# Attention and expert kernel: masked scores kept in SBUF, first weights split in two parts, first x loaded tile by tile

## What is computed

```python
latent = xn @ w_kv_down                      # rank 128
k, v   = split(latent @ w_kv_up)             # 16 heads of 64
q      = xn @ w_q
att    = softmax(causal(q @ k.T / 8))
y      = (att @ v) @ w_out
# ffn: router of 8 experts (top 2 of sigmoid scores), each expert silu(x@g.T)*(x@u.T)@d.T,
# plus one shared expert for all tokens
```

## Time and profile before

| | |
|---|---|
| time, median of 3 | 1002.02 us |
| the profiled execution's own time | 1002.06 us |
| its span, first to last instruction | 1000.3 us |
| PE busy | 957.1 us (96%) |
| DVE, ACT, POOL busy | 727.8, 635.1, 340.7 us |
| mean granted TensorE clock | 0.993 of full |

### The profile page before, as it was taken

How to read it: one execution, slowest core, us unless ns; L and a number is a source line. 1 busy time by engine, 2 the same in 40 slices (tenths; PEclk the granted TensorE clock), 3 DMA queues, 4 the chain that set the end, 5 groups by cost and what they waited for, 6 DMA issues and landing times.

```text
span 1000.3 us, 20204 instructions
## 1 busy us (share of the span) xinstructions
PE 957.1 (96%) x7200; PEld 768.1 (77%) x7200; DVE 727.8 (73%) x2014; ACT 635.1 (63%) x1799; POOL 340.7 (34%) x333
## 2 busy tenths in 40 slices
PE   3879997899999999999999999999999999999998
PEld 2656776678888878888788887888878778777776
DVE  4889699997666666675666656676675786888884
ACT  3746666554767666766666775666756676667772
POOL 0231113223234234442343523445131444444441
PEclk9899999999999999999999999999999999999999
DMA  6486424361324525455244553456433442533421
GB/s 192 164 305 243 161 98 147 126 205 36 135 76 147 185 91 174 123 180 178 101 162 142 180 161 105 153 165 178 152 97 134 161 125 76 180 108 101 132 86 43
DMA packets 65412, 142.78 MB, mean 143 GB/s; under 512 B 7776, under 2 KB 40288, under 8 KB 63520
## 3 DMA queue, kind: packets, MB, share of 16 engines
q1 hardware_dynamic: 52880, 92.19, 27.9%
q0 software_dynamic: 12432, 49.29, 15.8%
HBM read 104.76 MB, written 36.70 MB: 141 GB/s over the span
## 4 chain that ended last, share of the span: by engine, by line
PE 83%; DVE 7%; issue 7%; POOL 1%; DMA 1%; ACT 1%; POOLq 0%; DVEq 0%; SPq 0%
PE PS L667 15%; PE PS L709 14%; PE PS L668 13%; PE PS L669 13%; PE PS L700 13%; PE PS L690 12%; PE PS L816 2%; DVE acc L985 1%; PE PS L808 1%; DVE PS L1240 1%; DMA xs<-xs_scratch 1%; POOL rstd L1345 1%; PE PS L715 1%; DVE ohB L1204 0%; DVE acc L1164 0%
## 5 line engine op out<-in xcount | busy, mean ns | idle before, releaser
L923 ACT ACTIVATE pp<-PS,nmax 128x128 f32<-128x128 f32 (+3 forms) x512 | 263.6, 532 | 130.6 <-DVE nmax L1240 130.4
L1240 DVE CUSTOM_DVE_ANT_0 PS<-PS,maskw 128x128 f32<-128x128 f32 (+3 forms) x512 | 232.3, 522 | 5.0 <-PE PS L690 5.0
L1396 POOL TENSOR_TENSOR yy<-yf,yy 128x512 fp32r<-128x512 f32 x63 | 82.4, 1307 | 287.2 <-ACT yy L853 287.2
L700 PE MATMUL PS<-ident,pp 128*128 128x128 f32 x1280 | 165.2, 275 | 0.3 <-DVE qk L1137 0.2
L690 PE MATMUL PS<-qk 64*128 64x256 f32 (+2 forms) x1536 | 147.1, 337 | 12.8 <-DVE qk L1226 11.0
L700 PEld LDWEIGHTS PS<-ident,pp 128*128 128x128 f32 x1280 | 141.3, 141 | 15.4 <-issue 9.3
L709 PE MATMUL PS<-pt,vv 128*64 128x512 f32 (+3 forms) x1024 | 152.0, 439 | 0.1
L709 PEld LDWEIGHTS PS<-pt,vv 128*64 128x64 f32 x1024 | 67.8, 136 | 90.4 <-issue 72.3
L690 PEld LDWEIGHTS PS<-qk 64*128 64x128 f32 x1536 | 114.2, 190 | 28.8 <-issue 10.7
L853 ACT ACTIVATE pt<-PS 128x384 f32<-128x384 f32 (+1 forms) x215 | 108.7, 512 | 3.3 <-PE PS L700 3.1
L1246 DVE COPY pt<-PS 128x384 f32<-128x384 f32 x169 | 99.7, 591 | 12.7 <-PE PS L700 12.7
(11 more groups left out here) (169 smaller groups left out, 2075.0 us busy)
## 6 DMA issues: line engine op xcount, KB each, us to landing
rb<-rr_scratch SPq DMA_DIRECT2D x128, 128.0 KB
wr<-wm_scratch SPq DMA_DIRECT2D x16, 768.0 KB, 5.5
y_scratch<-acc SPq DMA_DIRECT2D x39, 256.0 KB
acc<-in_x SPq DMA_DIRECT2D x16, 512.0 KB, 5.6
wm_scratch<-hh SPq DMA_DIRECT2D x10, 768.0 KB, 4.0
xs_scratch<-wr SPq DMA_DIRECT2D x7, 1024.0 KB, 5.0
xs<-xs_scratch SPq DMA_DIRECT2D x7, 1024.0 KB, 4.8
xn_scratch<-acc SPq DMA_DIRECT2D x8, 512.0 KB, 3.0
```

What stands on the lines that cost most here:

```text
L700: done = e.transpose(o, pp[:, i % 4, P_AT[t] + 128 * kt:P_AT[t] + 128 * kt + 128], ident[:, :])
L923: e.activation(pp[:, b, P_AT[t]:P_AT[t] + n], g[:, at:at + n], ACT.Exp, scale=-1.0, bias=nmax[:, b, t:t + 1], accum_out=rs[:, i % 4, 2 * t ...
L1240: e.tensor_tensor_reduce(o, o, maskw[:, 512 - n:512], -1.0, 3e38, ALU.add, ALU.min, accum_out=nmax[:, b, t:t + 1]).then_inc(v_max, 1)
L1396: e.tensor_tensor(yy[:, i % 2, 1, :], yf[:, :], f32(yy[:, i % 2, 0, :]), ALU.subtract).then_inc(g_yl, 1)
```

## The change: what it does, and the diff

DVE's masked scores go to `pp` in SBUF instead of back to PSUM; ACT exponentiates them in place. A score bank is free when DVE is done, no longer when ACT is. `HELD` and three entries of `LAG` change. The weights that the first two pairs need (columns 0 to 255 of q, k and v: "A") are loaded and split first; the rest ("B") is loaded behind the second x and split in the tick of `norm_stats` 1. The first x comes in four tiles with a semaphore each. Router weights, mask, bias and router constants are loaded on ACT's queue, and DVE works on them after `vA`. The transposes of the normalized rows wait for one tile at a time.

```diff
-LAG = {... "y": 0, "yh": 4, ... "bt": 0, ...}
+LAG = {... "y": 1, "yh": 3, ... "bt": 2, ...}
-HELD = {... "scores": 3, ... "attend": 4, ...}
+HELD = {... "scores": 2, ... "attend": 3, ...}
+WEIGHT_PARTS = ("d", "kA", "qA", "vA", "qB", "kB", "vB")
@@ work_order
-    at(-9.9, "split_w", "k")
-    at(-8.9, "split_w", "v")
+    for u, name in ((-8.5, "vA"), (-1.3, "qB"), (-1.2, "kB"), (-1.1, "vB")):
+        at(u, "split_w", name)
...
     put("norm_scale", 0)
+    put("split_w", "kA")
+    put("split_w", "qA")
     for c in range(2):
         put("norm_rows", 0, c)
         tick()
-    put("split_w", "q0")
-    put("split_w", "q1")
@@ released_by
-            "scores": lambda P, jh: (a_exp, 8 * P + (2, 4, 5, 6, 7, 8)[jh]),
+            "scores": lambda P, jh: (v_max, 8 * P + (2, 4, 5, 6, 7, 8)[jh]),
@@ sync_program
-            e.dma_start(x_in(0), rows128(x[0])).then_inc(d_xin[0], 16)
+            for t in range(4):
+                e.dma_start(x_in(0)[:, t, :], x[0, 128 * t:128 * t + 128, :]).then_inc(d_x0[t], 16)
             e.dma_start(ident[:, :], consts[:, 0:128]).then_inc(d_ident, 16)
-            e.dma_start(gw[:, :, :], gate_w).then_inc(d_gw, 16)
-            e.dma_start(lb[:, :], lb_bias).then_inc(d_lb, 16)
-            e.dma_start(kc[:, :], consts[:, 384:672]).then_inc(d_kc, 16)
-            e.dma_start(hf[:, 0, :], consts[:, 800:1312]).then_inc(d_mask, 16)
-            for name in ("d", "q0", "q1", "k", "v"):
-                if name == "q0":
-                    w.wait_ge(d_xin[0], 16)
+            for name in WEIGHT_PARTS:
                 e.dma_start(raw_w[name][0], raw_w[name][1]).then_inc(d_wraw[name], 16)
-            e.dma_start(x_in(1), rows128(x[1])).then_inc(d_xin[1], 16)
+                if name == "vA":
+                    e.dma_start(x_in(1), rows128(x[1])).then_inc(d_xin[1], 16)
             def moe_load(q):
...
-                    w.wait_ge(v_wlo, whi_at["v"])
+                    w.wait_ge(v_wlo, whi_at["vB"])
@@ tensor_program
-                    w.wait_ge(v_wlo, whi_at["q1"])
+                    w.wait_ge(v_wlo, whi_at["qA" if p < 2 else "qB"])
...
-                    w.wait_ge(v_wlo, whi_at["k"])
+                    w.wait_ge(v_wlo, whi_at["kA" if p < 2 else "kB"])
...
-                    w.wait_ge(v_wlo, whi_at["v"])
+                    w.wait_ge(v_wlo, whi_at["vB" if g4 else "vA"])
...
-                    w.wait_ge(*scaled(i))
                     for t in range(4):
+                        w.wait_ge(v_xn, 4 * i + t + 1)
                         done = e.transpose(...)
@@ scalar_program
+            e.dma_start(gw[:, :, :], gate_w).then_inc(d_gw, 16)
+            e.dma_start(hf[:, 0, :], consts[:, 800:1312]).then_inc(d_mask, 16)
+            e.dma_start(lb[:, :], lb_bias).then_inc(d_lb, 16)
+            e.dma_start(kc[:, :], consts[:, 384:672]).then_inc(d_kc, 16)
...
-                            w.wait_ge(v_max, exps(2 * i + h, max(t, 1)))
-                            if i >= 2:
-                                w.wait_ge(p_T, 3 * (2 * (i - 2) + h) + min(t, 2) + 1)
-                            else:
-                                w.wait_ge(v_wlo, whi_at["q1"])
...
-                            e.activation(pp[:, b, P_AT[t]:P_AT[t] + n], g[:, at:at + n], ACT.Exp, ...)
+                            scores = pp[:, b, P_AT[t]:P_AT[t] + 128 * (t + 1)]
+                            w.wait_ge(v_max, exps(2 * i + h, t))
+                            e.activation(scores, scores, ACT.Exp, scale=-1.0, bias=nmax[:, b, t:t + 1],
@@ vector_program
-            w.wait_ge(d_gw, 16)
-            e.tensor_copy(gwH[:, :, :], gw[:, :, :]).then_inc(v_cst, 1)
-            w.wait_ge(v_cst, 1)
-            low(gwL[:, :, :], gw[:, :, :], gwH[:, :, :]).then_inc(v_cst, 1)
-            w.wait_ge(d_mask, 16)
-            e.tensor_copy(maskw[:, :], hf[:, 0, :]).then_inc(v_cst, 1)
...
                     low(oL, raw, oH).then_inc(v_wlo, 1)
+                    if i == "vA":
+                        w.wait_ge(d_gw, 16)
+                        e.tensor_copy(gwH[:, :, :], gw[:, :, :]).then_inc(v_cst, 1)
...
+                        e.tensor_copy(maskw[:, :], hf[:, 0, :]).then_inc(v_cst, 1)
...
+                            if i >= 2:
+                                w.wait_ge(p_T, 3 * (2 * (i - 2) + h) + min(t, 2) + 1)
+                            else:
+                                w.wait_ge(v_wlo, whi_at["qB" if i else "kA"])
-                            e.tensor_tensor_reduce(o, o, maskw[:, 512 - n:512], -1.0, 3e38, ALU.add, ALU.min,
+                            e.tensor_tensor_reduce(pp[:, b, P_AT[t]:P_AT[t] + n], g[:, at:at + n], maskw[:, 512 - n:512], ...
```

More of the change, by code:

```diff
@@ L46 @@
       "shared7": 248.0, "finish": (255.5, 257.2, 258.2), "fix": 8.0, "loading": 2.3, "xs": -9.4, "down": 4.6}
-HELD = {"finish": 57, "scores": 3, "transposes": 3, "attend": 4, "query": 1, "key": 2, "value": 4, "gate_up": 3,
+HELD = {"finish": 57, "scores": 2, "transposes": 3, "attend": 3, "query": 1, "key": 2, "value": 4, "gate_up": 3,
         "out_part": 1, "down": 3, "recip_rows": 3, "block_rows": 4}
@@ L299, in attention_moe_kernel @@
         part_d = nc.dram_tensor("part_scratch", [TOKENS, C], F32)
+        d_x0 = [new_sem(f"d_x0{i}") for i in range(4)]
         d_xin = [new_sem(f"d_xin{i}") for i in range(2)]
         d_ident, d_mask, d_gw, d_lb, d_kc = (new_sem("d_" + n) for n in ("ident", "mask", "gw", "lb", "kc"))
-        d_wraw = {n: new_sem("d_wraw_" + n) for n in ("d", "q0", "q1", "k", "v")}
+        d_wraw = {n: new_sem("d_wraw_" + n) for n in WEIGHT_PARTS}
         d_wout = new_sem("d_wout")
@@ L364, in attention_moe_kernel @@
                     fixed[NBATCH - 1, piece[2] // 2] = added[piece]
-        whi_at = {n: i + 1 for i, n in enumerate(("d", "q0", "q1", "k", "v"))}
+        whi_at = {n: i + 1 for i, n in enumerate(WEIGHT_PARTS)}
         group_of = {k: item[-1] for k, item in enumerate(items)}
@@ L436, in attention_moe_kernel @@
         xr_w = xr[:, :, :].rearrange("p a n -> p (a n)")[:, 0:768]
[L437 to L443, removed]
+        raw_k, raw_q = acc[:, 0, :, :].rearrange("p t n -> p (t n)"), pp[:, 2:4, 0:1024]
+        raw_v, q_in = xr[:, :, :].rearrange("p a n -> p (a n)"), w_q.rearrange("p (c n) -> p c n", c=2)
+        raw_w = {"d": (rb[:, 0:256], w_kvd) + tuple(a[:, :, :].rearrange("p c n -> p (c n)") for a in (wdH, wdL))}
+        for part, n in (("A", slice(0, 256)), ("B", slice(256, 1024))):
+            raw_w["k" + part] = raw_k[:, n], w_kvu[:, n], wkH[:, n], wkL[:, n]
+            raw_w["q" + part] = raw_q[:, :, n], q_in[:, :, n], wqH[:, :, n], wqL[:, :, n]
+            raw_w["v" + part] = raw_v[:, n], w_kvu[:, 1024 + n.start:1024 + n.stop], wvH[:, n], wvL[:, n]
         rank, steps, below, jc, pcol, iota, token = (kc[:, i:j] for i, j in (
@@ L479, in xs_ready, with x_loaded @@
             return (v_xtl, 2) if b < 1 else (d_xs, 16 * b)
+        def x_loaded(b, t):
+            return (d_xin[b % 2], 16 * ((b + 1) // 2)) if b else (d_x0[t], 16)
         def scaled(b):
@@ L910, in scalar_program @@
                     for h in range(2):
-                        g = bank(kind, i, 2 * j + h)
+                        b = 2 * (i % 2) + h
                         for t in S_tiles(j):
-                            n = 128 * (t + 1)
-                            at = 256 if t == 1 else 0
-                            b = 2 * (i % 2) + h
-                            w.wait_ge(v_max, exps(2 * i + h, max(t, 1)))
-                            if i >= 2:
-                                w.wait_ge(p_T, 3 * (2 * (i - 2) + h) + min(t, 2) + 1)
-                            else:
-                                w.wait_ge(v_wlo, whi_at["q1"])
+                            scores = pp[:, b, P_AT[t]:P_AT[t] + 128 * (t + 1)]
+                            w.wait_ge(v_max, exps(2 * i + h, t))
                             if i >= 4:
                                 w.wait_ge(v_rr, i - 3)
-                            e.activation(pp[:, b, P_AT[t]:P_AT[t] + n], g[:, at:at + n], ACT.Exp, scale=-1.0,
-                                         bias=nmax[:, b, t:t + 1],
+                            e.activation(scores, scores, ACT.Exp, scale=-1.0, bias=nmax[:, b, t:t + 1],
                                          accum_out=rs[:, i % 4, 2 * t + h:2 * t + h + 1]).then_inc(a_exp, 1)
@@ L1152, in vector_program @@
                     for t in range(4):
+                        w.wait_ge(*x_loaded(i, t))
                         e.bn_stats(st[:, t, :], a[:, t, :]).then_inc(v_st, 1)
```

13 lines of the change are left out of this document (8 added, 5 removed).

## The result

The changed kernel takes 996.82 us (median of 14 executions, 994.8 to 999.5), the kernel before beside it 1000.31 us (14, 998.49 to 1003.85): ratio 0.9964, 95% interval [0.9953, 0.9976], so 3.5 us or 0.36% faster. The prediction said 1004 us, slower by 2. The profiled execution took 996.82 us; its span is 995.0 us against 1000.3. The execution profiled before was 1.8 us above the median of this second set of runs, so about that much of the 5.3 us between the spans is no gain.

The account below looks back on a forecast made before the run. PE was taken as the bound from 300 to 800 us, so only the first 220 us could change, DVE being the bound for nearly 200 us. From 1002.06 us, +3 (start) and -1 (lags) gave 1004, range 996 to 1010.

Parts of the forecast that it names:

- rival (a): Chain behind the expert load covered, DVE's steps 0.3 us a pair shorter over 17 pairs (-5): 996 us, chance 0.23.
- The first x: Start of the kernel: x in tiles lands by 6.2 us, the latent starts at 12.5, not 15.63: -3.1 us.
- From latent to the first scores: Start, latent to DVE's first maximum: smaller splits, but router weights and mask added; net -0.9 us, maximum at 23.1.
- The second parts: Between pairs 0 and 1: splitting the B weights ahead of key 1's remainder eats the start's 4.0 us; net +0.3 us.
- What is queued behind them: Start to 100 us: first expert load issued later, delaying ACT, the store and the load of x 3: +3 us.
- Lags and banks: `y` one tick later removes DVE waits for PE: -1 us in DVE-bound time before 220 us; other lags nothing.
- rival (b): Banks counted free too early make PE wait in the full stretch, 0.1 us a pair over 60 pairs: 1010, chance 0.12.
- Scores in SBUF: DVE's masked-score step 0 to -38 ns each, taken as 0; ACT's exponentials +17 us in all, mostly hidden.
- Rival (c): Start's stall whole: load chain costs full 5 us, 1006; or x no sooner, 1005; both, 1007 to 1009; chance 0.25.

Follow-up runs that it names:

- start_alone: The kernel before with only the new start (x by tiles, weights in two parts, constants on ACT's queue): 1001.3 us against 1000.9, ratio 1.0008.
- bt_only: The kernel before with only the remainder of the expert blocks' rows (bt) two ticks later: 1019.9 us against 1020.2, ratio 0.9995.
- output_psum: The changed kernel with masked scores back in PSUM, read there by ACT, banks released by ACT: 997.5 us, ratio 0.9958 to the kernel before.

## Why the prediction was wrong

The time fell into the range, but on the other side of before, and not by the case that gave that number: that rival (a) has 996 us is luck. The forecast was +3 from the start and -1 from the lags between 100 and 220 us; the changed kernel's trace shows -1.2 at pair 5 and -3.9 behind it, of which 0.9 is the profiled execution's. Of the signs named for being wrong one came: the statistics of x 3 at 46.53 us, before 48.

- **"The first x", half right.** The forecast took the row of the whole x, 4.1 us to landing, for each tile; the first tile was there at 2.92 us, 2.2 us after the first issue, the fourth took 3.2 and landed at 5.3 (6.2 taken). Scaling began at 7.53 against 8.4 said, the latent at 11.7 against 12.5. The Trainium skill ("DMA: Bandwidth & Descriptors", the anatomy of one DMA) puts a tile at an estimated 2.3 us. The trace agrees with it for the first tile alone; the fourth lies between it and the row that I took.
- **"From latent to the first scores", mis-sized.** It was put at -0.9 us and measured -2.6: 8.9 us from the latent to the first maximum, 11.5 before. What goes beyond the 0.9 goes with the clock, which I did not price. In the changed kernel PE's 128x512 matmuls take 0.63 us up to 15.3 us and 0.40 behind; before they took 0.63 up to 21.1. Under the scores of pair 0 the granted clock was 0.57 before (24 to 28 us) and is 1.00 now (19 to 23 us), and the first maximum stands 1.1 us behind their start, not 1.8. So the first maximum came at 20.60 against 23.1, and the lead was 6.5 us, not 4.0.
- **"The second parts", right in the mechanism.** The lead is lost to them, at the place named: ACT's copies, DVE idle until then, three remainders, key 1, and the scaling of batch 1 in 1.37 us (1.4 said). With the lead 2.5 us larger the scores of pair 1 came at 33.10, not 36.1, and the first maximum of pair 1 at 34.75, not 37.9: -2.9 us against before, where +0.3 was said.
- **"What is queued behind them", the step that failed in the start.** Three terms of it were mis-sized: `vB` done at 32.4 (35.5 said), the expert load landed in 2.9 us (4.6 taken, the median over the whole run; the 3.5 of a quiet queue was named and not used, and before the same load took 2.9), and x 3's load 2.4 us behind the store (2.9 said). So ACT copied at 35.36 (40.1 said) and x 3 was issued at 40.55 (45.9). The wait for x 3 did not arise. The next x loads are waited for longer, the first 2.71 us at 59.77 against 1.66. From pair 1 to pair 5 the lead fell by 0.4 us, where +2.7 was said, and +3 became about zero: start_alone, 1.0008.
- **"Lags and banks", the step that failed behind it, and the one that decides.** I gave y -1 us, which the runs bear out (1.1 above the common 0.9), and put the bank counts at nothing, looking at them for danger alone, as rival (b). The smaller count made PE's banks come from other holders, and one of them, key 10's, was worth about 2 us. What would have told me was in the trace of before: at 185.84 us the same wait of 1.03 us for L1214 as in bt_only, a product waiting for an instruction whose data it does not read.
- **"Scores in SBUF", right in the time, wrong in the row.** DVE's form of 512 went from 727 to 686 ns, a little beyond my bound of -38 and far from the 0 that I took. ACT's exponentials are busy 17.1 us more, against 17 said, and their accumulator reads 11.6 less; ACT as a whole is busy 16.2 us more. Neither shows in the end, not even from 100 to 220 us: output_psum against the changed kernel.
- **Rival (a)** gave 996 us by a covered load chain and by DVE's shorter steps (-5). The first held in the main; the second did not: the steps are shorter, and no time comes of it. Its 17 pairs were too many as well: pair 17 starts at 303 us, and up to 220 us there are 11 pairs behind pair 0. **Rival (b)** did not arise: PE is at 100 of 100 us from 300 to 800. **Rival (c)** fell with the tiles landing early.

## What to carry to other kernels

Where a planner hands out a shared resource by due times, a changed lifetime of one kind reshuffles the holders of all. Look in the trace of before for waits whose releaser has nothing to do with the waiting instruction's data, and for small operations of DVE that take a microsecond too long beside one of POOL, and price the change by whether it moves those. And follow a lead from pair to pair before pricing the thing named in a change's title: here a start 6 us shorter came to nothing, since two more limits stood right behind it. And read the granted clock of each trace before comparing two: 6.8 us at half of it is worth 2 to 3 us here, as much as the thing under test.
